# Attention over 4 batches of 1024 positions on one core: splitting the value matmuls of three sets by quarter pairs and chunk pairs

## The reference, cut to what matters

```python
h = _group_norm(x, gn_w, gn_b)                       # 8 groups of 16 channels
q = jnp.einsum('oc,bcn->bon', qw, h) + qb[None, :, None]
k = jnp.einsum('oc,bcn->bon', kw, h) + kb[None, :, None]
v = jnp.einsum('oc,bcn->bon', vw, h) + vb[None, :, None]
attn = jnp.einsum('bcn,bcm->bnm', q, k) / jnp.sqrt(C)
attn = jax.nn.softmax(attn, axis=-1)
out = jnp.einsum('bnm,bcm->bcn', attn, v)
out = jnp.einsum('oc,bcn->bon', pw, out) + pb[None, :, None]
return x + out.reshape(B, C, H, W)
```

## Time and profile before

| | |
|---|---|
| median of three runs | 144.14 us (143.91 to 144.76) |
| the profiled execution's own time | 144.62 us |
| its span, first to last instruction | 142.6 us |
| outside the span | 2.0 us |
| TensorE matmuls busy | 130.1 us, 91% of the span, 647 instructions |
| VectorE busy | 99.5 us, 70% |
| ScalarE busy | 64.9 us, 46% |
| GpSimd busy | 26.1 us, 18% |
| DMA from `blocks` to `pT` | 112 issues of 128 KB |
| granted TensorE clock | 1.00 over the whole span |

### The profile page before, as it was taken

The page is one execution under the profiler, slowest core; times in us unless marked ns, Lnnn a source line. Parts: engine busy times, 40 slices in busy tenths (PEclk is TensorE's granted clock), DMA queues, the critical chain, the costliest instruction groups (busy, mean ns, idle before and its releaser), DMA issues.

```text
span 142.6 us, 2014 instructions
## 1 busy us (share of the span) xinstructions
PE 130.1 (91%) x647; PEld 109.4 (77%) x647; DVE 99.5 (70%) x172; ACT 64.9 (46%) x112; POOL 26.1 (18%) x33
## 2 busy tenths in 40 slices
PE   5999999997779999799999995999999969999990
PEld 5997878865558887688888883888888847988880
DVE  0577779989998679679697789366977893521222
ACT  4053789564566653544436845054543333512000
POOL 5043050930202061100050323000030030003000
PEclk9999999999999999999999999999999999999999
DMA  4950000005996799499824997899509987979211
GB/s 147 306 210 0 0 5 0 27 12 115 214 205 168 171 211 203 118 205 210 195 93 92 202 209 200 202 204 210 162 0 205 209 195 202 205 161 223 78 37 74
DMA packets 9565, 20.98 MB, mean 147 GB/s; under 512 B 2362, under 2 KB 4052, under 8 KB 9556
## 3 DMA queue, kind: packets, MB, share of 16 engines
q1 hardware_dynamic: 8816, 20.59, 59.3%
q10 hardware_dynamic: 740, 0.28, 0.7%
HBM read 4.07 MB, written 2.11 MB: 43 GB/s over the span
## 4 chain that ended last, share of the span: by engine, by line
PE 56%; SPq 19%; DVE 11%; issue 6%; DMA 5%; POOL 0%; DVEq 0%; POOLq 0%
PE ACC L377 20%; SPq L189 19%; PE S L322 6%; DMA pT<-blocks 5%; PE S L326 5%; PE S L323 5%; PE S L266 5%; DVE blocks L665 4%; DVE s_sb L656 4%; PE A L302 3%; PE ACC L350 2%; PE S L350 2%; PE A L404 1%; PE ACC L404 1%; DVE bn L581 1%
## 5 line engine op out<-in xcount | busy, mean ns | idle before, releaser
L377 PE MATMUL ACC<-pT,v 128*128 128x256 f32 x224 | 52.8, 381 | 4.1 <-DMA pT<-blocks 4.1
L656 DVE TENSOR_SCALAR_CACHE_REDUCE s_sb<-S,row_term 128x1024 f32<-128x1024 f32 x32 | 41.0, 1281 | 20.7 <-PE S L326 20.2
L377 PEld LDWEIGHTS ACC<-pT,v 128*128 128x128 f32 x224 | 41.2, 190 | 10.9 <-issue 5.6
L502 ACT ACTIVATE s_sb<-s_sb,rowmin 128x1024 f32<-128x1024 f32 x32 | 36.8, 1151 | 20.9 <-DVE s_sb L656 19.9
L665 DVE STREAM_TRANSPOSE blocks<-s_sb 128x1024 f32<-128x1024 f32 x28 | 34.7, 1240 | 0.0
L322 PE MATMUL S<-h_hi,g_hi 128*128 128x512 f32 x64 | 30.2, 472 | 0.3 <-issue 0.3
L323 PE MATMUL S<-h_lo,g_hi 128*128 128x512 f32 x64 | 25.2, 393 | 0.0
L326 PE MATMUL S<-h_hi,g_lo 128*128 128x512 f32 x64 | 19.9, 392 | 0.0
L810 POOL TENSOR_TENSOR xb<-rden_bc,xb 128x512 f32<-128x512 f32 (+1 forms) x7 | 8.4, 1194 | 53.0 <-DVE rden_bc L685 45.5
L326 PEld LDWEIGHTS S<-h_hi,g_lo 128*128 128x128 f32 x64 | 12.0, 188 | 2.8
L322 PEld LDWEIGHTS S<-h_hi,g_hi 128*128 128x128 f32 x64 | 12.1, 189 | 2.5 <-issue 0.4
(11 more groups left out here) (90 smaller groups left out, 103.4 us busy)
## 6 DMA issues: line engine op xcount, KB each, us to landing
pT<-blocks SPq DMA_DIRECT2D x112, 128.0 KB, 2.4
rden_bc<-row_store SPq DMA_DIRECT2D x6, 256.0 KB, 3.6
x_sb<-x SPq DMA_DIRECT2D x1, 1024.0 KB, 6.0
out<-xb SPq DMA_DIRECT2D x8, 128.0 KB, 2.8
out<-xb SPq DMA_DIRECT2D x4, 256.0 KB, 3.2
x_sb<-x SPq DMA_DIRECT2D x2, 256.0 KB, 3.0
x_sb<-x SPq DMA_DIRECT2D x1, 512.0 KB, 3.9
w_in<-weights ACTq DMA_DIRECT2D x2, 128.0 KB, 3.5
```

Of the source, the lines that this page charges most:

```text
L377: last = pe.matmul(to, v[:, b % 3, t, :], probs[:, :, t, :], start=(t == 0), stop=(t == KT - 1))
L502: act.activation(s_sb[:, c % 3, :], s_sb[:, c % 3, :], ACT.Exp, bias=rowmin[:, c % CH:c % CH + 1], scale=-1.0, accum_out=den[:, n % 2, k:k ...
L656: dve.tensor_scalar(s_sb[:, c % 3, :], S[:, c % 2, :], row_term[:, b % 2, i:i + 1], None, ALU.add, ALU.min, accum_out=rowmin[:, i:i + 1]). ...
```

## The change

In the three crossing sets the units are cut another way. `part` now picks the pair of quarters in every set, and in a crossing set `half` picks the pair of chunks (and with it the batch of v). A unit there takes all 8 key tiles in 128 columns (2 quarters x 64) where it took 4 key tiles in 256 columns (4 quarters x 64). Units 0 and 1 wait for quarters 0 and 1, units 2 and 3 for quarters 2 and 3, as in the other sets. The wait for v stands in each unit of a crossing set. The last unit that reads batch 0's v is then unit 8, not unit 7, so the wait of `copy_v` for batch 3 asks for one more finished unit (9).

```diff
             def moved_unit(n, u):
-                b, part, half = (FIRST[n] + u) // CH, u // 2, u % 2
+                part, half = u // 2, u % 2
+                b = FIRST[n] // CH + (half if crosses(n) else 0)
+                if half == 0 or crosses(n):
+                    pe.wait_ge(v_ready, VP * (b + 1))
                 if half == 0:
-                    pe.wait_ge(v_ready, VP * (b + 1))
...
-                    for a in range(NQ) if crosses(n) else (2 * part, 2 * part + 1):
+                    for a in (2 * part, 2 * part + 1):
                         pe.wait_ge(moved[n % 2][a], MOVED * ((n + 1) // 2))
-                probs = moved_view(n)
+                to = last_sums[part] if n == LS - 1 else sums[n][:, UW * part:UW * (part + 1)]
+                to = to.rearrange("p (a n) -> p a n", a=2)
+                probs = moved_view(n)[:, 2 * part:2 * (part + 1)]
+                tiles = range(PT * half, PT * (half + 1))
                 if crosses(n):
-                    cs = slice(2 * Q * part, 2 * Q * (part + 1))
-                    to = sums[n].rearrange("p (a n) -> p a n", a=NQ)[:, :, cs]
-                    probs = probs[:, :, :, cs]
...
-                for t in range(PT * half, PT * (half + 1)):
+                    cs = slice(2 * Q * half, 2 * Q * (half + 1))
+                    to, probs, tiles = to[:, :, cs], probs[:, :, :, cs], range(KT)
+                for t in tiles:
                     last = pe.matmul(to, v[:, b % 3, t, :], probs[:, :, t, :], start=(t == 0), stop=(t == KT - 1))
...
             def copy_v(b, k):
...
-                    act.wait_ge(part_done, CH * (b - 2))
+                    act.wait_ge(part_done, CH * (b - 2) + 1)
```

## The result

The changed kernel's runs took 140.34, 140.37, 140.73 and 141.05 us, median 140.55 us, against a median of 144.21 us for the kernel before on the same chips: a ratio of 0.975 (0.971 to 0.979), 3.7 us less. The profiled execution took 140.34 us with a span of 138.4 us. All four lay in the forecast range of 139.0 to 141.7 us; the central value of 139.8 us was 0.75 us too low.

What follows compares the result with a forecast made beforehand. TensorE, busy 130.1 of 142.6 us, was taken as the bound, with three waits for DMA issuing. -4.76 us (waits) + 0.4 (narrow matmuls) = -4.3 us: median from 144.14 to 139.8 us, range 139.0 to 141.7.

Steps and rivals of the forecast that it cites:

- The waits: TensorE's stands before unit 0 of sets 2, 4 and 6 cost 1.15, 1.76 and 1.85 us; all 4.76 us go.
- The condition in time: Quarters 0 and 1 of sets 2, 4 and 6 land before unit 0 starts, with over 2 us to spare.
- The narrow matmuls: Twelve units with 192 records of 128 columns at 110.5 ns, for 96 at 216.3 ns, cost +0.4 us (-0.2 to +0.7).
- The cover: In the narrow units, 96 more weight loads of 190 ns each stay hidden beside the matmul before.
- The extra of 25 ns a record: Estimate from the Trainium skill for 192 new value-matmul records: 4.8 us, the whole gain; as a rival, chance 0.02.
- What is late next: g_lo for L302 in steps 15 and 23 keeps 0.7 us; set 7's quarters for its unit 0 keep 0.4 to 1.3.
- Issuing or bytes: At the three stands TensorE waits for SyncE's queue to issue DMAs, some 0.63 to 0.69 us each, not for their bytes.
- From span to median: The profiled execution, 144.62 us, lay 0.48 above the median; its forecast of 140.3 us became a median of 139.8 us.
- The rivals: Four other outcomes: new wait 0.15, narrow matmuls slower 0.04, fixed cost per load and matmul 0.02, no earlier landing 0.02.
- A wait takes their place: Rival: g_lo in steps 15 and 23, or set 7's quarters, come late, 1 to 1.5 us, 141.1 us; chance 0.15.
- The 234 ns: Pace of the first 18 records of 128 columns; would make +24 us, left out as belonging to the first 6 us alone.

## Why the prediction was right, and where it was off

**The waits.** Right in place, cause and size. Whole steps gave 4.76 us. The changed kernel has none of them, the kernel with the wait moved and the wide units kept gains as much, and the four-quarter wait put back loses the gain. By the sums over steps above the changed kernel is 4.76 - 0.65 = 4.1 us shorter. The span fell by 4.2 us; the rest is the start, 0.13 us earlier at step 14.

**The condition in time.** Right. Quarters 0 and 1 had landed at 52.24, 81.57 and 110.93 us, the units began at 56.72, 85.72 and 113.55: 2.6 us or more to spare, though the long issue took 0.9 us off set 6's margin. Three quarters would have been early enough for sets 2 and 4 and just not for set 6.

**The narrow matmuls.** The term "+0.4 us" was mis-sized within its own bounds of 0.2 to 0.7: 0.65 us. It took the mean of the pace of L404 (109 ns) and of L302 (112 ns), and the units run at L302's: 1.78 us over 16 records is 111 ns. That is the pace of weight loads of 190 ns, which L302 and L377 share, and the run at 64 columns shows it again, at 111 to 112 ns with half the columns. The transposes' loads last 140 ns in the same trace and come every 109. L302 alone was the right row.

**The cover.** "They are hidden as long as a load runs beside the matmul before it" was almost right. A load does run beside each matmul, but the loads come every 112 ns and half of a wide record is 108, so at 128 columns they already set the pace, by those 3 to 4 ns. The extra of 25 ns a record, which the prediction estimated from the Trainium skill, was not there: 0.65 us over 192 records are 3.4 ns.

**What is late next.** Right. L302 waits for no g_lo in steps 15 and 23, set 7's issues began at 116.22 us (forecast near 116.2) and its unit 0 at 124.47 (forecast about 124.5) without a wait. The eight transfers that it needs had landed at 123.73 us, a margin of 0.7 us where 0.4 to 1.3 was forecast.

**Issuing or bytes.** "For the issuing of DMAs, not for their bytes" was right for the pace of the queue, and too strong for the stand: halving the bytes took 1.6 us off it, most of it through a faster landing.

**From span to median.** This is the step that missed most. The forecast for an execution like the profiled one was 140.3 us and the changed kernel's took 140.34. That close an agreement is partly luck: the matmuls cost 0.25 us more than the sum had, and part of it was given back by a start that was 0.13 us earlier for no reason of the change. Then 0.48 us were taken off, because the profiled execution of before lay that far above its median. That median came from three runs; over the sessions it was 144.2 to 144.7 us, and the changed kernel's profiled execution lay 0.2 us below its own median, not above it. So the 0.48 was scatter. With +0.65 for the matmuls and without that step the forecast is 144.62 - 4.76 + 0.65 = 140.5 us.

**The rivals.** None came in. "A wait takes their place" had its evidence in the profile, but its margins held.

## What to carry to other kernels

A consumer that waits for a whole series of transfers waits for the issue of the last one. Cut the work so that its first part needs the first transfers, or put other work in front of it; here both gave 3.5 to 3.7 us. Price the cut by the row that is nearest in kind, its weight load included, and do not go below the width at which a load takes as long as its matmul, in this kernel 128 float32 columns. Read a wait from whole steps with and without it, and carry the profiled execution's time over to the median of many runs, not of three.

## What the runs showed of the hardware that was not expected

- A longer stand can cost more than its length. Behind idle times of 0.7 to 1.6 us the granted clock stayed at 1.00 in every profiled execution. Behind 2.76 and 3.18 us it fell to about half for the unit that followed; behind 2.99 us it did not. Most executions were not profiled, but ten of the twelve of the two kernels with such a stand have a mean clock of 0.984 to 0.988, so the fall is the common case and not a certain one. With the wide units these are 1.6 to 2.3 us slower than the one execution without the fall, with the narrow ones, in the second session, 0.7 to 0.8 us.
- The first microseconds ran at the pace of the lower level, though the page shows a granted clock of 1.00 there, and so does the table ahead of the prediction. The narrow unit behind the long stand took 3.32 us to the start of what follows, 207 ns a record. The very first matmuls start 213 ns apart. The trace's list of granted clocks begins only at 6.46 us (at 5.25 us in the changed kernel's trace), and where it has no entry the page shows 1.00. After that point ten records of the same line and shape take 112 ns each, in the chain of the kernel before:

```profile
9.14 1.12 PE S L266 x10
```

  In the changed kernel's trace the faster pace began 1.2 us sooner, and the first eighteen took 4.01 us instead of 4.21. The 234 ns that the prediction left out of its range were thus the price of that pace, and not of 128 columns.
- An issue of SyncE's queue takes 0.59 us, but now and then one takes 1.0 to 2.2 us, and the traces tell at what moments. The pages of before and after count a few packets of the kind "instruction" on a queue of their own:

```profile
q8 instruction: 5, 0.08, 0.2%
```

```profile
q8 instruction: 6, 0.10, 0.3%
```

  Each moves 16 KB. In the thirteen kept traces 39 issues of L189 take over 0.95 us, and every one of them overlaps in time with such a packet, though these packets fill under 5% of the spans. Where they fall hangs on the program: the fourth issue of set 6 took 1.48 to 1.95 us in all five traces with twelve narrow units of 128 columns (the changed kernel's two, the three-quarter wait's and the four-quarter wait's two), and 0.59 us in all four traces with wide units and sixteen issues a set. So the long issue that made the four-quarter wait longer goes with the narrow cut. The changed kernel has it too, and there it costs nothing because of the margin. That the packets hold up the issue is the likely reading; how they would do it is not shown.
- The changed kernel therefore also took away a risk. The four-quarter wait with the same code costs 7 to 8 us more than the two-quarter one (147.7 and 148.3 against 140.6 us), not 4.8, since a long issue, a longer stand and, in most executions, a lower clock add up.
